# A perceiver-style twelve-sublayer kernel: small-head scores in halves, three layers turned before their norm, another order

## The reference, cut to what matters

```python
x = x + _L0_xattn_ref(ctx_1024, _layernorm(x), ...)   # 16 heads of 64, latents attend to context and themselves
x = x + _L0_attn_ref(_layernorm(x), ...)              # gated recurrence ("rnn")
x = x + _L0_ffn_ref(_layernorm(x), ...)               # base linear + top-2 of 8+2 low-rank experts ("lora")
x = x + _L1_xattn_ref(_layernorm(x), ctx_1024, ...)   # one-head cross attention ("x1")
x = x + _L1_attn_ref(_layernorm(x), ...)              # causal linear attention, 16 heads of 8 ("lin")
x = x + _L1_ffn_ref(_layernorm(x), ...)               # causal softmax attention, 16 heads of 8, and 4 experts ("m1", "rms")
x = x + _L2_xattn_ref(ctx_1024, _layernorm(x), ...)   # 8 heads of 64 ("x2")
x = x + _L2_attn_ref(_layernorm(x), ...)              # softmax attention in a window of 64, 16 heads of 8 ("loc")
x = x + _L2_ffn_ref(_layernorm(x), ...)               # top-1 of 8 experts with a capacity ("m2")
x = x + _L3_xattn_ref(_layernorm(x), ctx_1024, W, b)  # x1 @ W1.T + mean over the context @ W2.T + b ("x3")
x = x + _L3_attn_ref(_layernorm(x), ...)              # convolution and state space ("ssm")
x = x + _L3_ffn_ref(_layernorm(x), ...)               # top-1 of 8 experts ("m3")
```

## Time and profile before

| | |
|---|---|
| time, median of 3 runs | 2597.32 us (2591.3 to 2600.08) |
| the profiled execution: time, span | 2592.37 us, 2590.6 us |
| PE busy | 2377.2 us, 92% of the span |
| DVE, ACT, POOL busy | 1463.5, 1179.5 and 940.0 us (56%, 46%, 36%) |
| mean granted PE clock | 0.98 of full speed |
| instructions | 41480, of them 16402 on PE |

### The profile page before, as it was taken

How to read it: one execution, slowest core, us unless ns; L and a number is a source line. 1 busy time by engine, 2 the same in 40 slices (tenths; PEclk the granted TensorE clock), 3 DMA queues, 4 the chain that set the end, 5 groups by cost and what they waited for, 6 DMA issues and landing times.

```text
span 2590.6 us, 41480 instructions
## 1 busy us (share of the span) xinstructions
PE 2377.2 (92%) x16402; PEld 1577.3 (61%) x16402; DVE 1463.5 (56%) x3815; ACT 1179.5 (46%) x2940; POOL 940.0 (36%) x860
## 2 busy tenths in 40 slices
PE   8999989989999999898999988989999999999898
PEld 5665656655666665565666665556666666656555
DVE  5446565565465566556553556656556455664634
ACT  4534344446445434444645343444454445354433
POOL 5324263342333335334232344433423133544300
PEclk9999999999999999999999999999999999999989
DMA  5000000000000000000000000000000000000000
GB/s 224 1 1 1 1 9 1 9 9 9 9 1 9 1 1 9 1 17 1 9 9 9 1 1 9 1 1 17 5 1 9 5 1 1 1 1 1 1 1 9
DMA packets 6098, 26.54 MB, mean 10 GB/s; under 512 B 656, under 2 KB 656, under 8 KB 5136
## 3 DMA queue, kind: packets, MB, share of 16 engines
q1 hardware_dynamic: 5904, 23.89, 2.5%
HBM read 21.79 MB, written 2.10 MB: 9 GB/s over the span
## 4 chain that ended last, share of the span: by engine, by line
PE 68%; DVE 20%; ACT 5%; issue 4%; POOL 4%; DMA 0%; POOLq 0%; DVEq 0%; SPq 0%; ACTq 0%
PE ps L461 9%; PE ps L478 7%; PE ps L516 6%; PE ps L492 6%; PE ps L835 4%; PE ps L582 4%; PE ps L484 3%; PE ps L561 3%; PE ps L446 3%; PE ps L559 3%; PE ps L556 2%; DVE P L1331 2%; PE ps L604 2%; DVE small L1318 2%; POOL small L1774 2%
## 5 line engine op out<-in xcount | busy, mean ns | idle before, releaser
L1798 POOL TENSOR_TENSOR P<-P,small 128x384 f32<-128x384 f32 x384 | 320.7, 857 | 564.6 <-DVE small L1356 564.6
L1077 ACT ACTIVATE P<-ps,small 128x192 f32<-128x192 f32 x768 | 313.7, 422 | 178.4 <-DVE small L1348 177.4
L1774 POOL TENSOR_TENSOR small<-small,mhalf 128x4 f32<-128x4 f32 x112 | 128.1, 1144 | 614.2 <-DVE small L1336 472.1
L478 PE MATMUL ps<-kvT,big 128*128 128x192 f32 x1536 | 304.3, 336 | 18.0 <-ACT P L1077 9.7
L1348 DVE TENSOR_REDUCE small<-ps 128x2 f32<-128x384 f32 x384 | 210.3, 552 | 128.4 <-PE ps L478 121.4
L478 PEld LDWEIGHTS ps<-kvT,big 128*128 128x128 f32 x1536 | 244.8, 190 | 58.3 <-ACT P L1077 36.3
L461 PEld LDWEIGHTS ps<-wts,P 128*128 128x128 f32 x1920 | 231.9, 192 | 47.3 <-issue 32.8
L461 PE MATMUL ps<-wts,P 128*128 128x128 f32 x1920 | 251.7, 280 | 5.9 <-DVE P L1717 3.5
L1888 POOL TENSOR_TENSOR P<-T 128x512 f32<-128x512 f32 x96 | 126.4, 1317 | 187.4 <-ACT T L1220 108.7
L492 PE MATMUL ps<-value,big 128*128 128x128 f32 x1536 | 188.8, 276 | 2.5 <-DVE big L1388 2.5
L484 PE MATMUL ps<-cst,P 128*128 128x128 f32 x1152 | 168.2, 278 | 23.9 <-POOL P L1798 11.0
(11 more groups left out here) (276 smaller groups left out, 4513.6 us busy)
## 6 DMA issues: line engine op xcount, KB each, us to landing
ctok<-ctok_dram SPq DMA_DIRECT2D x8, 512.0 KB, 3.5
ctxT<-ctx_dram SPq DMA_DIRECT2D x8, 512.0 KB, 3.5
big<-fold_dram SPq DMA_DIRECT2D x3, 1024.0 KB, 9.3
wts<-weights_dram SPq DMA_DIRECT2D x1, 2530.0 KB, 24.5
wts<-weights_dram SPq DMA_DIRECT2D x1, 2189.0 KB, 19.0
X<-x_dram SPq DMA_DIRECT2D x8, 256.0 KB, 3.0
out_dram<-X SPq DMA_DIRECT2D x8, 256.0 KB, 2.0
wts<-weights_dram SPq DMA_DIRECT2D x1, 1536.0 KB, 28.8
```

The source lines that it names most:

```text
L478: m = pe.matmul(ps[s][:, at:at + KEYS], big[s][:, BANK * b + 128 * p:BANK * b + 128 * p + 128], kvT[s][:, keys_at(b):keys_at(b) + KEYS], s ...
L1077: m = act.activation(probs(s, b // 2)[:, to:to + KEYS], ps[s][:, at:at + KEYS], ACT.Exp, bias=small[s][:, 4 * e + p:4 * e + p + 1], accum_ ...
L1774: pool.tensor_tensor(rstd(s, name, n), variance(s, name, n), mhalf[:, 0:n], ALU.pow).then_inc(*sig("rstd", s))
L1798: m = pool.tensor_tensor(view, view, over(small[s][:, at:at + 2], 2, [128, 2, KEYS]), ALU.mult)
```

## The change

Four edits.

1. **Scores in halves.** In `m1` and `loc` each of the two banks of eight heads has signals of its own. PE makes and releases the scores of one half (still all its products), DVE takes maximum and difference of 512 columns twice in place of 1024 once, ACT takes the exponential of 512 columns twice. A half of the next tile's scores waits only for its own half's difference, a half's transposes only for its own half's exponential.
2. **Residual turned unscaled.** In `lora`, `m2` and `x3` PE transposes `X` itself. It is let go by the first tile's `bn_stats` (which stands behind the add on DVE), not by `rescale`. The inverse root is applied later: to the logits (one small DVE product), and to the layer's result, which is added by four scaled adds (`add_scaled`; so it was in `m2`, and is new in `lora` and `x3`). In `m2` it is folded into the gate by one more 128x4 product.
3. **The context's mean ahead.** The sum over the context and its product with `x3b` move from `x3` into `loc`: the sum stands between the variance and `rescale` of `loc`, the product in bank 0 once the last scores are subtracted. DVE adds the bias row `b3` to it while it moves it to SBUF, and in `x3` adds that to the residual. POOL's preset in `x3` goes.
4. **Another order.** All five bit strings are new.

The diff, cut to its core:

```diff
 ORDER = dict(
-    pe=(2463, int(""
-        "24401810708420a600fe0080201002679ebaf56750430d5f1afdc5c65caad6194a0a45053d3cf942650eb07a38148059b8b2"
+    pe=(2519, int(""
+        "8110060860105200802804020427df78ef5d6d750430bb779f3e4327165671e240a4500a0f9ef54480240480bdad65e94233"
...
+        GROUP = dict(lin=0, m1=1, loc=2)
+        HALVES = dict(m1=4, loc=12)
...
                 def softmax_heads(s, i, name, causal):
-                    def scores(t):
-                        for hf in range(2 if causal else 0):
+                    def scores(t, hf):
+                        p0 = 64 * hf
+                        if causal:
                             pe.matmul(bank(s, hf), ident_b[:, :], over(causal_b[:, :], 1, [128, 8, SEQ]), start=True, stop=False)
...
+                    def next_scores(t):
                         for hf in range(2):
-                    def next_scores(t):
-                        yield
-                        pe.wait_ge(*on("n_sub", s, i, u0 + t - 1))
-                        pe.wait_ge(*on("bd_ready", s, i, 3 * GROUP[name] + t - 1))
-                        scores(t)
+                            yield
+                            if hf == 0:
+                                pe.wait_ge(*on("bd_ready", s, i, 3 * GROUP[name] + t - 1))
+                            pe.wait_ge(*on("n_sub", s, i, HALVES[name] + 2 * t - 2 + hf))
+                            scores(t, hf)
...
-                            if hf == 0:
-                                pe.wait_ge(*on("n_exp", s, i, v0 + t))
+                            pe.wait_ge(*on("n_exp", s, i, 2 * v0 + 2 * t + hf))
...
-                    pe.wait_ge(*on("tok", s, i, "lora"))
-                    turn(s, 0, N[s])
+                    pe.wait_ge(*on("tok", s, i, "lora.r"))
+                    turn(s, 0, res(s, i))
...
                     yield from softmax_heads(s, i, "loc", False)
+                    yield
+                    pe.wait_ge(*on("n_sub", s, i, HALVES["loc"] + 2 * TILES - 1))
+                    pe.wait_ge(*on("x3_sum", s, i))
+                    for t in range(TILES):
+                        for bb in range(2):
+                            mean_b = small[s][:, MEAN + 8 + 2 * t + bb:MEAN + 9 + 2 * t + bb].to_broadcast([128, SEQ])
+                            m = pe.matmul(part(s, 0, t)[64 * bb:64 * bb + 64, :], mean_b, W("x3b"), start=True, stop=True)
+                    m.then_inc(*sig("y_ps", s))
...
                     def exps(t):
-                        yield
-                        act.wait_ge(*on("n_sub", s, i, u0 + t))
-                        act.activation(sco(s, t), sco(s, t), ACT.Exp, scale=HD ** -0.5).then_inc(*sig("n_exp", s))
+                        for hf in range(2):
+                            yield
+                            act.wait_ge(*on("n_sub", s, i, HALVES[name] + 2 * t + hf))
+                            half = sco(s, t)[:, 512 * hf:512 * hf + 512]
+                            act.activation(half, half, ACT.Exp, scale=HD ** -0.5).then_inc(*sig("n_exp", s))
...
-                def moments(s, name, src):
+                def moments(s, name, src, raw=False):
                     for t in range(TILES):
                         m = dve.bn_stats(bn(s, name, t), tile_of(src, t))
+                        if raw and t == 0:
+                            m.then_inc(*sig("tok", s))
...
+                def late_norm(s, i, name):
+                    yield
+                    moments(s, name, res(s, i), raw=True)
+                    dve.tensor_scalar(variance(s, name), mean_var(s, name)[:, :, 1], EPS5, None, ALU.add).then_inc(*sig("var", s))
...
+                    if late:
+                        dve.wait_ge(*on("rstd", s, i, name))
+                        link(dve.tensor_tensor(route(s, L, e), found.rearrange("p (t e) -> p t e", e=16)[:, :, 0:e],
+                                               over(rstd(s, name), 2, [128, TILES, e]), ALU.mult))
...
-                    yield from add_biased(s, i, "lora", 0)
+                    yield
+                    dve.wait_ge(*on("x_biased", s, i, "lora"))
+                    dve.wait_ge(*on("y_ps", s, i, "lora"))
+                    link(add_scaled(s, i, 0, lambda t: rs(s, "lora", t)))
...
                     def minus_max(t):
-                        yield
-                        dve.wait_ge(*on("n_s", s, i, u0 + t))
-                        sc = bank(s, 0, 2).rearrange("p (h k) -> p h k", k=SEQ)
-                        link(dve.tensor_reduce(small[s][:, 0:16], sc, AX.X, ALU.max))
+                        for hf in range(2):
+                            yield
+                            dve.wait_ge(*on("n_s", s, i, HALVES[name] + 2 * t + hf))
+                            sc, top = bank(s, hf).rearrange("p (h k) -> p h k", k=SEQ), small[s][:, 8 * hf:8 * hf + 8]
+                            link(dve.tensor_reduce(top, sc, AX.X, ALU.max))
...
                 def concat(s, i):
-                    link(dve.tensor_reduce(small[s][:, 0:8], ctxT[s][:, :].rearrange("p (b k) -> p b k", k=CTX), AX.X, ALU.add))
-                    dve.tensor_scalar(small[s][:, 8:16], small[s][:, 0:8], 1.0 / CTX, None, ALU.mult).then_inc(*sig("x3_sum", s))
-                    yield from rescale(s, i, "x3", N[s], res(s, i))
-                    yield from add_biased(s, i, "x3", 1)
+                    yield from late_norm(s, i, "x3")
+                    yield
+                    dve.wait_ge(*on("zT_ps", s, i, "x3"))
+                    link(dve.tensor_tensor(res(s, i), tmp(s, 2), res(s, i), ALU.add))
+                    yield
+                    dve.wait_ge(*on("rstd", s, i, "x3"))
+                    dve.wait_ge(*on("y_ps", s, i, "x3"))
+                    link(add_scaled(s, i, 1, lambda t: rs(s, "x3", t)))
```

More of the change, by code:

```diff
@@ L84 @@
[L84 to L89, removed]
@@ L119 @@
 VARS = ["rnn", "lora", "x1", "lin", "m1", "rms", "x2", "loc", "m2", "ctx0", "ctx1", "x3", "ssm", "m3", "x0"]
-TOKENS = ["rnn", "lora", "lora.c", "x1", "lin", "m1", "rms", "m1.c", "x2", "loc", "m2", "m2.oh", "m2.x", "ctx0", "ctx1",
-          "x3", "ssm", "m3", "m3.oh", "x0"]
+TOKENS = ["rnn", "lora.r", "lora.c", "x1", "lin", "m1", "rms", "m1.c", "x2", "loc", "m2.r", "m2.oh", "m2.x", "ctx0", "ctx1",
+          "x3.r", "ssm", "m3", "m3.oh", "x0"]
 TURNS = ["lat", "rnn", "lora", "lora.c", "x1", "lin", "lin.y", "m1", "m1.y", "rms", "x2.c0", "x2.c1", "x2",
@@ L127 @@
 FIRST = [(0, "lat")] + [(-1, n) for n in AHEAD]
-SUMS = ["rnn", "lora", "x1", "lin", "m1.y", "loc", "m2", "x3", "ssm", "m3"]
+SUMS = ["rnn", "lora", "x1", "lin", "m1.y", "x3.m", "loc", "m2", "x3", "ssm", "m3"]
 LOGITS = ["lora", "m1", "m2", "m3"]
-BIASED = ["h0", "lora", "x1", "loc", "x3"]
+BIASED = ["h0", "lora", "x1", "loc"]
 PROJ = ["lin", "lin.v", "m1", "m1.p1", "m1.v", "loc", "loc.v"]
@@ L906, in concat @@
                     yield
[L907 to L908 removed]
+                    pe.wait_ge(*on("tok", s, i, "x3.r"))
+                    turn(s, 0, res(s, i))
                     yield
                     pe.wait_ge(*on("zT", s, i, "x3"))
[L911 to L918 removed]
+                    tokens(s, 1, [(Z[s], W("x3a"))]).then_inc(*sig("y_ps", s))
                 def ssm(s, i):
@@ L1484, in lora @@
                 def lora(s, i):
-                    yield from norm(s, i, "lora", res(s, i), N[s], weights_centred=True)
+                    yield from late_norm(s, i, "lora")
                     yield
-                    link((yield from router(s, i, "lora", 10, 2)))
+                    link((yield from router(s, i, "lora", 10, 2, late=True)))
                     yield
@@ L1632, in local @@
                 def local(s, i):
-                    yield from norm(s, i, "loc", res(s, i), N[s], weights_centred=True)
+                    yield
+                    moments(s, "loc", res(s, i))
+                    dve.tensor_scalar(variance(s, "loc"), mean_var(s, "loc")[:, :, 1], EPS5, None, ALU.add).then_inc(*sig("var", s))
+                    link(dve.tensor_reduce(small[s][:, MEAN:MEAN + 8], ctxT[s][:, :].rearrange("p (b k) -> p b k", k=CTX), AX.X, ALU.add))
+                    dve.tensor_scalar(small[s][:, MEAN + 8:MEAN + 16], small[s][:, MEAN:MEAN + 8], 1.0 / CTX, None, ALU.mult)\
+                       .then_inc(*sig("x3_sum", s))
+                    yield from rescale(s, i, "loc", N[s], res(s, i))
                     yield
```

119 lines of the change are left out of this document (61 added, 58 removed).

## The result

The changed kernel takes 2617.24 us (median of four runs, 2614.92 to 2618.84) against 2594.31 us for the kernel before beside it (2590.66 to 2600.08). The ratio is 1.0082, with a 95% interval of 1.0067 to 1.0097: slower by over 0.3%, some 21 us by the ratio, where 22 us less were forecast. The profiled execution took 2618.48 us, with a span of 2616.6 us and a mean clock of 0.980, the clock of before.

A forecast was written before the change was run, and what follows sets the result against it. PE was taken as the bound, busy 2377.2 of 2590.6 us, gains lying in its 213.4 us without a matmul and its clock. Terms -6 - 7 - 8 - 4 - 6 + 8 + 1 = -22 us took 2597.3 to 2575 us (2560 to 2588).

The forecast's parts named there:

- Late turns: PE's 12 waits before turns of lora, m2 and x3, 7.4 us together, shrink to 1.4 us: -6 us.
- the router of `m2`: One-hot and gate in m2 start 3 us sooner, cutting 12.0 us of PE waits: -7 us, between -3 and -12.
- The order: New order gives more cover before turns of the other nine layers, 42.5 us of waits: -8 us, 0 to -15.
- Halves: In the score steps, a first half's exponential starts earlier; half of 8.5 us of waits go: -4 us, 0 to -8.
- The clock: PE's granted clock recovers 12% of 52 us lost, as idle time shrinks: -6 us, between -2 and -12.
- DVE's extra work: 42.6 us added on DVE by halved passes, scaled adds and bias, partly in the path: +8 us, +3 to +20.
- Table loads: Eight more table loads on ACT, 10.3 us, mostly hidden: +1 us, at worst +10.
- the one on the slower side: ACT's table loads and extra DVE passes lie bare: +12 us, about 2609 us; chance 0.16.
- The rival by which the wait only moves: Turns come early, but router and final adds still wait for POOL's root: about 2594 us; chance 0.17.
- two rivals: One is the wait that moves; the other says shorter slot paths win more, -45 us, 2552 us, chance 0.20.

The follow-up runs named there:

- joint_products: The changed kernel, but PE makes both masks and all four score products of a tile in one step; DVE and ACT stay in halves: 2587.92 us, ratio 0.9969.
- late_old_order: The kernel before, old order, with only lora and m2 turned from the unscaled residual and the inverse root applied later: 2593.81 us, ratio 0.9993.
- late_halves_old_order: The kernel before, old order, with late norm in lora and m2 and halves on DVE and ACT, PE's products together: 2599.59 us, ratio 1.0040.
- unsplit_new_order: The changed kernel with halves undone on PE, DVE and ACT, each at its second half's place; the rest kept: 2581.87 us, ratio 0.9949.
- masks_between: The kernel before, with m1's mask of the second half moved between the two pairs of score products: 2626.19 us, ratio 1.0108.
- joint_loc_only: The changed kernel, but with PE's four score products of a tile in one step in loc only: 2605.81 us, ratio 1.0020.

## Why the prediction was wrong

The step that failed stands in its first paragraph: "The change leaves PE's products as they are: the mask, score and `x3b` products are the same in number and shape, only regrouped or earlier." Number and shape did stay, and the groups confirm it. The regrouping was the cost. It gave the score lines 52.3 + 5.4 = 57.7 us of PE's time, and 1.1% of the kernel's. No term of the sum and no rival held it: `joint_products` has 0.9969 where the change has 1.0082, with nothing but the split undone. The rows to see it were in the trace of before: 512 instructions of 646 ns in a busy time of 73.6 us can only be had with four or more at a time. I had not divided the one by the other.

A second step failed behind it. Even with the products together the change gives 8 us (0.31%), not 22, and PE is idle 220.6 us, not 197. Parts 1 to 4 took the waits that they name to be gained; the runs show that shorter waits at the turns came back as waits at other places, and that the gain came for the most part with the clock (0.984).

1. *Late turns, -6 us*, and 2. *the router of `m2`, -7 us.* The waits behaved: none of PE's waits for `rescale` stands before these turns, as there is no `rescale` there, the gate went from 8.8 to 3.1 us, and the new wait is 3.8 us where under 3 was said. As time they are worth nothing in the old order (`late_old_order`), where the gate waits 11.8 us. If they pay with the order, no run shows it by itself.
3. *The order, -8 us.* Waits before the other turns were to fall from 42.5 to some 34.5 us and fell to 31.1. The count of cover at 72 places was good. With the edits in `x3` the order is worth 0.7%, some 18 us (`late_halves_old_order` to `joint_products`). It can't be set against the -8 us alone, since in the sum parts 1, 2 and 5 lean on the new order too. And it is not made of this part's waits: PE's idle time rose by 3.5 us in that step.
4. *Halves, -4 us.* Wrong sign. The waits for the differences did fall by 6.3 us, but behind PE's slower products; with those together they are 19.6 us. On DVE and ACT alone the halves cost 11 us in the old order and, by `joint_products` against `unsplit_new_order`, 0.2% (+-0.2) in the new one.
5. *The clock, -6 us.* The mean stayed 0.980, and the window from 2470 us fell to 0.74. Fewer idle microseconds did not mean a better clock in the changed kernel. From `late_halves_old_order` to `joint_products` the clock went from 0.977 to 0.984 with no fewer of them. To tie the clock to the sum of the idle time was wrong in both.
6. *DVE's extra work, +8 us, at worst +20.* The busy time came as counted (+21.0 us), and the 11 us of the halves are inside the range.
7. *Table loads, +1 us.* Eight more, 34 in all, and hidden; waits on exponentials and Gelus went from 9.7 + 6.8 to 10.8 + 7.7 us.

Of the rivals, the one on the slower side gave a time near the result (2609 us), for the wrong reason: it was to decide by table loads and DVE's passes, and the runs show neither as the cause. PE's idle time fell by 23.7 us, where about 16 (213 to 197) were forecast. That it fell was luck, since slower products cover waits: with the products together PE is idle 220.6 us. The rival by which the wait only moves is what the late norm does in the old order: waits before turns fall by 5.7 us there, the gate's rise by 3.0, and the time stays. It is also nearest to `joint_products`, where idle time left the turns and came back elsewhere. The sums of two rivals don't come out as written: 24 + 8 + 4 + 6 is 42 us and not 45, with parts 6 and 7 left out, and -6 - 2 + 8 leaves 2597 us and not 2594. Neither moves the forecast.

What stays open: why `joint_products` and `unsplit_new_order` have the better clock, and why the clock differs between executions of one kernel; how the new order and `x3`'s edits share their gain; and a form of halves that keeps all four quarters of the array busy, which wasn't tried.

## What to carry to other kernels

Before you split a step of small products in two, look at which of them run beside each other: compare the sum of their durations with the busy time of their line. Products on different parts of the array belong next to each other in the program, and the split must leave each piece with all parts, or it costs what it cost here: twice the time at the same count of instructions. And do not take less idle time for a gain as long as busy time has grown: a slower engine covers the waits on all others. Last, look at the granted clock of every execution before a few microseconds are put down to an edit.

## What the runs showed of the hardware

Four fp32 products of 64 rows, 64 columns and 512 moving columns, one on each quarter of the array, take 1.09 us together; two of them on one half of the rows take 1.08 us. One full-array mask product between the two pairs is enough to part them (`masks_between`: +35.1 us over 32 tiles). If nothing stands between the pairs they run together, even where they come from separate steps of the program with separate signals (the row at 1251.83 us).

The mean granted clock does not follow the sum of PE's idle time: 217.1 us idle with 0.977 (`late_halves_old_order`), 220.6 us with 0.984 (`joint_products`). It also differs between executions of one kernel, and the time with it: 0.980 with 2591.96 us to 0.990 with 2573.57 us (`unsplit_new_order`), 0.978 with 2614.2 us to 0.987 with 2594.3 us (`joint_loc_only`).

A table load takes 1.28 us, and the instruction behind it can start right after it: in the kernel before, the load at 1363.49 us is followed by its Gelu at 1364.78 us.
